# Attention and MLP block on one core: fewer key columns per matmul, keys split over two token halves, a shared copy of the values, and a new order of the work

## The reference

```python
xw = windows of 7x7 tokens of x                      # 32*64 windows, 49 tokens, 96 channels
xn = layernorm(xw) * ln_g + ln_b
q, k, v = split(xn @ qkv_w.T + qkv_b)                # 12 heads of 8
attn = softmax(q * 8**-0.5 @ k.T + bias_table[REL_IDX])
seq = x + (attn @ v) @ proj_w.T + proj_b
bn = batchnorm(depthwise_conv3x3(seq))
out = bn + gelu(bn @ w1.T + b1) @ w2.T + b2          # hidden 384, exact gelu
```

## Time and profile before

| | |
|---|---|
| three timed runs, median (lowest to highest) | 3189.77 us (3189.08 to 3205.73) |
| the profiled execution | 3164.1 us, its span 3162.3 us |
| granted TensorE clock, mean | 0.993 |
| busy share PE / PEld / DVE / ACT / POOL | 96% / 67% / 91% / 88% / 62% |
| DMA, hardware queue of SP | 198.40 MB, 22.6% of 16 engines |

### The profile page before, as it was taken

The page is one execution under the profiler, slowest core; times in us unless marked ns, Lnnn a source line. Parts: engine busy times, 40 slices in busy tenths (PEclk is TensorE's granted clock), DMA queues, the critical chain, the costliest instruction groups (busy, mean ns, idle before and its releaser), DMA issues.

```text
span 3162.3 us, 199772 instructions
## 1 busy us (share of the span) xinstructions
PE 3029.4 (96%) x88076; PEld 2105.9 (67%) x88076; DVE 2888.8 (91%) x4908; ACT 2768.5 (88%) x4867; POOL 1956.6 (62%) x2574
## 2 busy tenths in 40 slices
PE   3899999999999999999999999999999999999997
PEld 2666666666766666666666666666666676666663
DVE  4799999999999999999999999999999999999996
ACT  2799999989989999998989999988989999998986
...
GB/s 40 86 91 96 91 96 94 92 95 91 97 91 94 95 94 95 96 91 95 91 96 94 94 96 94 92 96 91 95 95 93 96 97 93 95 98 91 95 92 41
DMA packets 269922, 288.31 MB, mean 91 GB/s; under 512 B 55651, under 2 KB 252580, under 8 KB 269062
## 3 DMA queue, kind: packets, MB, share of 16 engines
q1 hardware_dynamic: 236294, 198.40, 22.6%
...
## 4 chain that ended last, share of the span: by engine, by line
PE 91%; issue 3%; ACT 2%; SPq 1%; DMA 1%; DVE 1%; POOL 0%; POOLq 0%; ACTq 0%; DVEq 0%
PE d_ps L255 21%; PE st_ps L299 12%; PE o_ps L345 11%; PE sm_ps L320 10%; PE b_ps L363 7%; PE b_ps L399 6%; PE a_ps L255 4%; PE b_ps L255 4%; PE a_ps L266 3%; PE a_ps L268 3%; PE a_ps L267 3%; PE d_ps L266 1%; PE d_ps L268 1%; PE b_ps L267 1%; PE d_ps L267 1%
## 5 line engine op out<-in xcount | busy, mean ns | idle before, releaser
L764 DVE SCALAR_TENSOR_TENSOR s<-ximg,cols,s 96x392 f32<-96x392 f32 x1792 | 1137.0, 635 | 30.7 <-POOL s L627 3.2
L738 DVE TENSOR_REDUCE mx<-sm_ps 128x12 f16<-128x588 f32 x1024 | 785.0, 767 | 127.7 <-PE sm_ps L320 125.1
L474 ACT ACTIVATE p<-st_ps 128x588 f32<-128x588 f32 x1024 | 672.4, 657 | 179.2 <-PE st_ps L299 176.1
L637 POOL DMA_DIRECT2D ox<-o_sb x1024 | 582.7, 572 | 30.8 <-ACT o_sb L499 17.2
L320 PEld LDWEIGHTS sm_ps<-k_all,q_all 127*49 127x49 f16 x24576 | 460.6, 104 | 171.5 <-issue 76.0
L255 PE MATMUL d_ps<-g,w_s 128*64 128x392 f32 x3072 | 560.2, 500 | 0.0
L299 PEld LDWEIGHTS st_ps<-q_all,k_all 128*49 128x49 f16 x24576 | 435.5, 103 | 157.2 <-issue 107.8
L610 POOL TENSOR_TENSOR s<-ximg,cols 96x392 f32<-96x392 f32 x256 | 216.0, 844 | 520.5 <-DVE y L801 519.9
L299 PE MATMUL st_ps<-q_all,k_all 128*49 128x49 f16 x24576 | 516.1, 186 | 21.4 <-issue 19.3
L320 PE MATMUL sm_ps<-k_all,q_all 127*49 127x49 f16 x24576 | 508.6, 186 | 25.9 <-issue 15.6
L599 POOL TENSOR_TENSOR xl<-xn,xh 96x392 f16<-96x392 f32 x256 | 258.8, 1011 | 273.6 <-ACT xh L555 256.5
...
## 6 DMA issues: line engine op xcount, KB each, us to landing
ox<-o_sb POOLq DMA_DIRECT2D x1024, 73.5 KB
k_all<-kh SPq DMA_DIRECT2D x512, 75.0 KB
q_all<-qh SPq DMA_DIRECT2D x512, 75.0 KB
x_sb<-in_x SPq DMA_DIRECT2D x256, 147.0 KB, 2.4
out<-y SPq DMA_DIRECT2D x256, 147.0 KB, 2.7
q_all<-ql SPq DMA_DIRECT2D x256, 75.0 KB
k_all<-kl SPq DMA_DIRECT2D x256, 75.0 KB
q_all<-mxt SPq DMA_DIRECT2D x256, 9.4 KB, 2.1
```

The costliest lines, as they stand in the source:

```text
L474: af(p32[:, p, :, :].rearrange("p (b h) n -> p b h n", b=2), st_ps[:, :, 0:HALF].rearrange("p b (h n) -> p b h n", n=TOK), ACT.Exp).then_i ...
L637: nc.gpsimd.dma_start(ox[:, c % 2, x4, :], o_sb[x4::4, c % 2, :, :]).then_inc(o_in[c % 2], 16)
L738: v.tensor_reduce(mx[:, c % 2, 0:HEADS, p].rearrange("p (b h) -> p b h", b=2), sm_ps[:, :, 0:HALF].rearrange("p b (h n) -> p b h n", n=TOK ...
L764: v.scalar_tensor_tensor(acc, image_rows(c, k // 3, k % 3), cw_c[:, k:k + 1], acc, ALU.mult, ALU.add)\
```

## The change

Queries and a third of the keys (heads 0 to 3, 32 columns) come out of one matmul with 128 stationary columns into `a_ps`; the other 64 key columns are made in two token halves (`token_halves_three`): the first 196 columns of tokens into partitions 0 to 63 of `b_ps`, the last 196 into partitions 64 to 127. So `kh` and `kl` are 128 x 200, and ACT's `key_high` and DVE's `key_low` handle 196 elements a partition and not 392. The terms go out in 12 transfers a chunk. The values go to `b_ps`, and are copied without a mask by ACT (second window of each pair, `upper_values`) and then DVE (first window). `projection` and `hidden` use 64-column halves; `projection`, `hidden` 0 and `second` now use `a_ps`, `hidden` 1 `b_ps`, `hidden` 2 `d_ps`. The maxima's transpose takes 48 columns and not 96. The order of every engine's queue is new, and there is one step more.

The diff, cut to its core (in the lists of calls and in SP's helpers the removed lines are left out; they stand in the kernel above, and what is left is the new order):

```diff
 TERMS = 4 * HD
+K_WITH_Q = 4
+ARRIVALS = 12
-STEPS = CHUNKS + 11
+STEPS = CHUNKS + 12
...
-        qh, ql, kh, kl = (sb(n, [C, 2, NW * KP], F16) for n in ("qh", "ql", "kh", "kl"))
+        qh, ql = (sb(n, [128, 2, NW * KP], F16) for n in ("qh", "ql"))
+        kh, kl = (sb(n, [128, 2, NP * KP], F16) for n in ("kh", "kl"))
...
+        def own_values(c, w):
+            return v32[64 * w:64 * w + 64, c % 2, :, :, :].rearrange("p h n (d x) -> p (h n d) x", x=4)[:, :, w]
...
+            def claim_terms(c):
+                if not real(c):
+                    return
+                wait(sp, sm_done[3], c - 4)
+                wait(sp, st_done[3], c - 4)
+            def query_term(n, part, done, c):
                 if not real(c):
                     return
                 wait(sp, done, c)
+                sp.dma_start(q_all[n:TERMS:4, c % 4, :, :], part[0:C, c % 2, :]).then_inc(exp_in[c % 4], 16)
+            def third_of_keys(n, part, done, c):
+                if not real(c):
+                    return
+                wait(sp, done, c)
+                sp.dma_start(k_all[n:TERMS:4, c % 4, 0:K_WITH_Q, :], part[C:128, c % 2, :]).then_inc(exp_in[c % 4], 16)
+            def rest_of_keys(n, part, done, c):
+                if not real(c):
+                    return
+                wait(sp, done, c)
+                for i in range(2):
+                    sp.dma_start(k_all[n:TERMS:4, c % 4, K_WITH_Q:, i * NP * KP:(i + 1) * NP * KP],
+                                 part[64 * i:64 * i + 64, c % 2, :]).then_inc(exp_in[c % 4], 16)
...
             for s in range(STEPS):
+                maximum_row(s - 6)
+                claim_terms(s - 4)
+                rest_of_keys(0, kh, kh_done, s - 4)
+                rest_of_keys(1, kl, kl_done, s - 4)
+                rest_of_keys(2, kh, kh_done, s - 4)
+                third_of_keys(2, qh, qh_done, s - 4)
+                query_term(2, ql, ql_done, s - 4)
+                third_of_keys(0, qh, qh_done, s - 4)
+                query_term(1, qh, qh_done, s - 4)
+                third_of_keys(1, ql, ql_done, s - 4)
                 load(s)
+                store(s - 12)
+                query_term(0, qh, qh_done, s - 4)
...
+            def token_halves_three(o, sh, sl, mh, ml):
+                terms = ((sh, mh), (sh, ml), (sl, mh))
+                for i, (s, m) in enumerate(terms):
+                    for h in range(2):
+                        last = mm(o[64 * h:64 * h + 64], s, m[:, NP * h:NP * h + NP], start=i == 0, stop=i == 2)
+                return last
...
                 if p == 0:
-                    wait_ring(pe, exp_in, c, 6 * 16)
+                    wait_ring(pe, exp_in, c, ARRIVALS * 16)
...
             def queries(c):
                 if not real(c):
                     return
                 wait(pe, xl_done, c)
-                free(pe, (g_done[1], c-7), (v32_done, c-2), (ql_done, c-1))
-                halves_three(a_ps[0:128, 0:CT], wq_h[:, 0:128], wq_l[:, 0:128], xh[:, c % 2, :, 0:TOK], xl[:, c % 2, :, 0:TOK]).then_inc(q_done, 1)
+                free(pe, (y_done, c-7), (g_done[0], c-7), (sum_done, c-5), (ql_done, c-1))
+                whole_three(a_ps[:, 0:CT], wq_h[:, 0:128], wq_l[:, 0:128], xh[:, c % 2, :, 0:TOK], xl[:, c % 2, :, 0:TOK]).then_inc(q_done, 1)
...
             def keys(c):
                 if not real(c):
                     return
                 wait(pe, xl_done, c)
-                free(pe, (g_done[2], c-7), (sum_done, c-5), (lnv_done, c), (kl_done, c-1))
-                halves_three(b_ps[0:128, 0:CT], wq_h[:, 96:224], wq_l[:, 96:224], xh[:, c % 2, :, 0:TOK], xl[:, c % 2, :, 0:TOK]).then_inc(k_done, 1)
+                free(pe, (g_done[1], c-7), (v32_done, c-2), (lnv_done, c), (kl_done, c-1))
+                token_halves_three(b_ps[:, 0:NP * TOK], wq_h[:, 128:192], wq_l[:, 128:192], xh[:, c % 2, :, 0:TOK], xl[:, c % 2, :, 0:TOK]).then_inc(k_done, 1)
...
-                free(pe, (ql_done, c+1), (g_done[1], c-6), (v32_done, c-1))
+                free(pe, (lnv_done, c+2), (kl_done, c+1), (g_done[1], c-6), (v32_done, c-1))
                 for n in range(NP):
                     s_h, s_l = (t[0:C, c % 2, 2 * n:2 * n + 2, :].rearrange("c w n -> c (w n)") for t in (xh, xl))
-                    last = whole_three(a_ps[:, 0:NP * C].rearrange("p (h n d) -> p n h d", n=NP, d=HD)[:, n], s_h, s_l,
+                    last = whole_three(b_ps[:, 0:NP * C].rearrange("p (h n d) -> p n h d", n=NP, d=HD)[:, n], s_h, s_l,
                                       wq_h[0:C, 2 * C:], wq_l[0:C, 2 * C:])
...
+                free(pe, (ql_done, c+4), (y_done, c-3), (g_done[0], c-3), (sum_done, c-1))
                 for w in range(2):
-                    o = b_ps[0:C, 0:CT].rearrange("c (r n w k) -> c w n r k", r=WS, w=2, k=WS)[:, w]
-                    last = mm(o, wp[:, 0:C], ox[:, c % 2, w, :].rearrange("c (n r k) -> c n r k", n=NP, k=WS), start=True, stop=True)
+                    o = a_ps[0:128, 0:CT].rearrange("c (r n w k) -> c w n r k", r=WS, w=2, k=WS)[:, w]
+                    last = halves(o, wp[:, :], ox[:, c % 2, w, :].rearrange("c (n r k) -> c n r k", n=NP, k=WS))
...
-            hidden_ps = {0: d_ps, 1: a_ps, 2: b_ps}
+            hidden_ps = {0: a_ps, 1: b_ps, 2: d_ps}
...
-                    free(pe, (xn_done, c+7), (y_done, c-1), (g_done[0], c-1))
+                    free(pe, (sum_done, c+2), (ql_done, c+6), (y_done, c-1), (g_done[0], c-1))
                 elif k == 1:
-                    free(pe, (v32_done, c+5), (ql_done, c+6), (g_done[1], c-1))
+                    free(pe, (v32_done, c+5), (lnv_done, c+7), (kl_done, c+6), (g_done[1], c-1))
                 elif k == 2:
-                    free(pe, (sum_done, c+2), (lnv_done, c+7), (kl_done, c+6), (g_done[2], c-1))
-                whole_three(hidden_ps[k][:, 0:CT], w1_h[:, k * 128:(k + 1) * 128], w1_l[:, k * 128:(k + 1) * 128], sh[:, :], sl[:, :]).then_inc(hid_done[k], 1)
+                    free(pe, (xn_done, c+7), (g_done[2], c-1))
+                halves_three(hidden_ps[k][:, 0:CT], w1_h[:, k * 128:(k + 1) * 128], w1_l[:, k * 128:(k + 1) * 128], sh[:, :], sl[:, :]).then_inc(hid_done[k], 1)
...
+                    free(pe, (g_done[0], c), (sum_done, c+2), (ql_done, c+6), (y_done, c-1))
+                halves(a_ps[0:128, 0:CT], w2_s[:, k, :], g[:, k, :], start=k == 0, stop=k == 1).then_inc(s_done[k], 1)
             for s in range(STEPS):
+                projection(s - 6)
+                exp_scores(s - 4, 1)
+                values_times_p(s - 5, 2)
+                values_times_p(s - 5, 3)
+                values(s - 3)
+                hidden(s - 8, 0)
+                max_scores(s - 3, 2)
+                hidden(s - 8, 2)
+                hidden(s - 8, 1)
+                values_times_p(s - 4, 0)
+                values_times_p(s - 4, 1)
+                max_scores(s - 3, 3)
+                second(s - 8, 0)
+                second(s - 8, 2)
+                maxima_rows(s - 3)
                 exp_scores(s - 4, 2)
+                second(s - 8, 1)
+                keys(s - 1)
+                centred(s)
                 exp_scores(s - 4, 3)
                 max_scores(s - 2, 0)
+                queries(s - 1)
+                variance(s)
+                exp_scores(s - 3, 0)
                 max_scores(s - 2, 1)
...
                 af(kh[:, c % 2, :].rearrange("c (w t) -> c w t", t=KP)[:, :, 0:TOK],
-                   b_ps[0:C, 0:CT].rearrange("c (w t) -> c w t", t=TOK), ACT.Identity, scale=1 / UP).then_inc(kh_done, 1)
+                   b_ps[:, 0:NP * TOK].rearrange("c (w t) -> c w t", t=TOK), ACT.Identity, scale=1 / UP).then_inc(kh_done, 1)
...
+            def upper_values(c):
+                if not real(c):
+                    return
+                wait(act, v_done, c)
+                wait(act, pv_done[3], c - 2)
+                af(own_values(c, 1), b_ps[64:128, 0:NP * C], ACT.Identity, scale=1 / UP).then_inc(upper_done, 1)
...
             for s in range(STEPS):
+                input_high(s - 1)
+                gelu(s - 8, 1)
                 if real(s - 8):
                     act.preload_act_table_set("natural_log_exp_and_others")
+                exp(s - 4, 2)
+                log_sums(s - 5)
+                key_high(s - 1)
+                inverses(s - 5)
+                square(s)
                 exp(s - 4, 3)
                 query_high(s - 1)
+                outputs(s - 4, 0)
                 exp(s - 3, 0)
+                log_variance(s)
+                root(s)
                 exp(s - 3, 1)
                 outputs(s - 4, 1)
+                upper_values(s - 2)
                 if real(s - 7):
                     act.preload_act_table_set("gelu_and_others")
                 gelu(s - 7, 0)
+                gelu(s - 7, 2)
...
                 to_channels(s - 4)
+                second_product(s - 5)
                 input_low(s)
+                image_high(s - 6)
+                first_product(s - 5)
```

(31 more changed lines are left out.)

112 lines of the change are left out of this document (19 added, 93 removed).

## The result

The changed kernel takes 3423.2 us (median of 4 runs, 3418.8 to 3429.2) against 3191.9 for the kernel before on the same chip: 1.0717 of it, 95% interval 1.0681 to 1.0753. The forecast was 3126 us, 0.98. It is wrong in sign and by some 300 us. The profiled execution of the changed kernel took 3425.3 us. The profiled execution of before, 3164.1 us, was shorter than all its timed runs, so distances taken from its profile are some 0.1 us a step too kind to it ((3191.9 - 3164.1) / 256); the ratios are not.

A forecast was written before the change was run, and what follows sets the result against it. PE was taken as the bound; with PE alone at 11.54 us and loop (c) at 11.65, a step of 11.66 against 11.91 was forecast: -0.25 x 256 = -64 us, 3189.8 to 3126 us, range 3075 to 3195.

The forecast's parts named there:

- loop (a): Values' product, ACT's copy, DVE's copy, then hidden 1: 1.29 us against 1.36 of cover on PE, cost 0 to 0.2.
- PE alone: PE's step without waits for other loops: floor 11.18 us plus 0.36 of stalls, 11.54.
- (c): SP's queue: twelve terms delay the store, block_out waits for its landing; a loop of two steps, 23.3 us, 11.65 a step.
- the last term: query_term(0), issued last in SP's queue: lands some 12.2 us after the keys, needed at about 12.9.
- PE's floor: PE's own start-to-start distances in a step: from 11.56 to 11.18 us, sum -0.38, bounds +0.05 and -0.48.
- Keys -0.25: On PE, three key pairs of 196 columns in token halves take 0.27 us, saving 0.25 a step.
- Projection -0.12: On PE, the projection in column halves, with the maxima block ahead: 1.15 to 1.03 us, bounds 0 and -0.16.
- Hidden exit -0.09: On PE, from the hidden layer's last matmul to the next block: 0.173 us as a pair instead of 0.26.
- Loop (b): Loop through DVE, POOL and PE's second layer: one step, 11.4 us; DVE's load falls from 11.28 to 10.7.
- the rival for "slower": SP's queue becomes the bound: from 0.76 us an issue slower than before, at 0.80 a time of 3239 us; chance 0.11.
- handoffs pile up: Rival: four loops within 0.3 us hit PE in turn; step 11.80 to 11.90, 3160 to 3187 us; chance 0.17.
- the +0.04: On PE, nine hidden pairs at 0.173 us for nine whole matmuls at 0.17: +0.04 a step at most.

The follow-up runs named there:

- e9: e5 with DVE's part of the values' copy ahead of tap 3 instead of behind it: 1.0166 of the kernel before.
- e18: e9 with the hidden layer in whole tiles again, as in the kernel before: 1.0071 of the kernel before.
- e2: The changed kernel with both copies of the values started by the product, DVE no longer waiting for ACT: 1.0615 of the kernel before.
- e1: The changed kernel with the store of a chunk issued one step earlier in SP's queue: 1.0505 of the kernel before.
- e5: e3 with the last query term ahead of load and store in SP's queue: 1.0248 of the kernel before.
- e3: The changed kernel with e1's early store and e2's parallel copies of the values together: 1.0401 of the kernel before.

## Why the prediction was wrong, step by step

Two steps failed. The values' copy of loop (a) was priced at 0.48 + 0.55 us and takes 0.87 + 0.83. And the near-equal loops were combined as a maximum plus 0.12 ("PE alone gives 11.54, (c) 11.65 ... I take 11.66"), where their losses add: the store, the copy and the last term, taken away one by one, gave back 2.1, 1.0 + 0.8 and 1.5 points.

**PE's floor: 11.18 forecast, about 11.35 left** (e9's shortest step, 11.60, less its wait for `maxima` 2, 0.18, and less 0.07 of the wait described next; a difference, not a step that ran). Keys -0.25: right. Projection -0.12: right or better. It is 0.68 itself (1351.76 to 1352.44), for 0.74 before. The block ahead of it takes 0.39 (1351.37 to 1351.76) and not the 0.32 of the forecast, but that is a wait: the projection now writes `a_ps`, which `query_low` has to have read (`ql_done` in its `free`). DVE in the same step of the changed kernel, and DVE and PE in a step of e9 where `query_low` was early:

```profile
1351.06 0.55 DVE L812 SCALAR_TENSOR_TENSOR ql<-a_ps,qh 128x392 f16<-128x392 f32 x1
```

```profile
675.86 0.57 DVE L815 SCALAR_TENSOR_TENSOR ql<-a_ps,qh 128x392 f16<-128x392 f32 x1 [0.37 <-ACT qh L551]
...
677.22 0.48 PE L354 MATMUL sm_ps<-k_all,q_all 127*49 127x49 f16 x24
677.54 0.86 PE L281 MATMUL a_ps<-ox,wp 96*64 96x196 f32 x8
```

`ql` ends at 1351.61 and the projection starts 0.15 later, and so it does in 144 of 146 steps of the changed kernel (600 to 2500 us); where `ql` ended early, the scores have their 0.32. The wait lists don't name it, the gaps are short. On average it costs 0.15 us a step, 0.10 in e9 and 0.11 in e18. The forecast's three loops have no term for this bank, and no run took the wait away.

Hidden exit -0.09: it was nothing, since the next block is values times P in 32-column tiles, which costs the same 0.26. And the sentence "the second layer, scores, values and variance keep their instructions" left out that their neighbours change: `max_scores` 0 ahead of the whole queries has 0.41 (1349.34 to 1349.75) and not 0.32, `exp_scores` 1 ahead of values times P 0.45 (0.41 before). The eight score blocks together cost 0.17 more, the 0.07 of the wait included. One gain was not seen: `mx` has 48 columns now, so the transpose fits into a half and costs next to nothing. The changed order was priced block by block where the price lies between blocks.

**Loop (a), 1.29 against 1.36: failed in its terms.** The halved copies were priced by the elements, from `kh` and `kl` (0.48, 0.55). They take 0.87 and 0.83, 1.8 with handoffs, so that `hidden` 1 starts 2.03 after the last start of the values (1354.03 to 1356.06) where 1.29 was forecast: half the partitions and half the elements save DVE 0.13 of 0.96. Price: 1.0 point as long as they run in turn (e2), 0.8 more for its place behind tap 3 (e9).

**Loop (c), 11.65: mechanism right, terms too small.** The price of an issue, on which the rival for "slower" hung, was right or better: 0.61 to 0.71. The store is issued 9.7 us after the keys on average (forecast 9.4), lands in 3.2 (2.7), and `block_out` starts 13.6 after the keys, where 12.1 was forecast. The loop of two steps was also closed with PE's 8.3 of an undisturbed step, though PE had its waits of loop (a) in there. Price: 2.1 points (e1). The forecast named the last term too ("lands some 12.2 after the keys and is needed at about 12.9") and took a margin of 0.7 us for enough: 1.5 points (e5).

**Loop (b), DVE's load: mis-sized.** DVE was to fall from 11.28 to 10.7 a step; it is 2910.8 / 256 = 11.37. The copy saved 0.13 instead of 0.4, `kl` its 0.2; but the taps went from 0.635 to 0.692 (7 x 0.057 = 0.40), `normalise` from 0.56 to 0.83. (These add to 0.34 a step, the busy time to 0.09: the durations of neighbours overlap more than before.) A tap of the short step above beside POOL's work, first DVE, then POOL:

```profile
1355.86 0.58 DVE L804 SCALAR_TENSOR_TENSOR s<-ximg,cols,s 96x392 f32<-96x392 f32 x1
...
1357.05 1.23 DVE L804 SCALAR_TENSOR_TENSOR s<-ximg,cols,s 96x392 f32<-96x392 f32 x1
```

```profile
1356.99 0.86 POOL L659 TENSOR_TENSOR part<-ximg,cols 96x392 f32<-96x392 f32 x1
```

The tap takes 0.58 alone and 1.23 when it starts just behind `part`. The Trainium skill, "SBUF — State Buffer", section "SBUF: two separate sides", has such a pair (DVE with two SBUF inputs, POOL reading SBUF) exclude each other for a whole instruction; the trace agrees roughly: the tap takes 0.65 us more than alone, of the 0.80 in which `part` was running, and ends 0.43 after it. Forecasts of DVE's time must ask what POOL does beside it. Worth 0.6 points on e3, nothing on e9.

**The sum.** Starting from +7.2%: store 2.1, copies in turn 1.0, last term 1.5, copy behind tap 3 0.8, hidden halves 1.0; 0.7 are left. By the ratio that is 0.09 us a step (the mean distances, 12.11 and 11.91, say 0.2, 0.1 of it for the short profiled execution of before). The projection's wait for `query_low`, 0.11 a step, is as much as that; beside it PE's weights wait for the maximum row's DMA (80.8 us in all), for the exponentials (68.9), for `maxima` 3 (60.9) and for the variance's input (48.3). Which of these would come back as time isn't known. So the forecast's rival "handoffs pile up" was right in kind; 0.17 was too little, and its price (11.80 to 11.90) far too low. The forecast took the largest of several loops within 0.3 us of each other and added 0.12. They were dearer, and they add up. Its own test ("wrong if the smallest step is not below 11.4, or if waits for DVE or a DMA stand above issue") came out against it on both counts: 11.99, and in PE's list 87.6 us for the values' copy (DVE `v`) against 35.4 for the longest "issue". In its sum the lower bound of the floor, -0.48, keeps the +0.04 that is "at most"; with 0 it is -0.52, which changes nothing here.
